# Attention scores from two float32r parts, two heads side by side in the row halves, and a regrouped first stage

## The reference

```
x = layernorm(x + attn(x));  x = layernorm(x + xattn(x, ctx));  x = layernorm(x + ffn(x))
attn:  q, k, v = x W^T + b per head; rotary turn of q and k; softmax(q k^T / 4) v, causal; output projection + bias
xattn: qp = x Wq^T; for each token the context row (of 1601) with the largest qp . ctx is chosen,
       mk, mv = split(ctx[chosen] Wkv^T): one key and one value shared by all heads, 16 wide
       softmax over the chosen rows (one per token, so a row counts as often as it is chosen); projection
ffn:   8 experts (4 x 256 and 4 x 512 wide), top 2 by sigmoid, relu squared, weighted sum
```

## Time and profile before

| engine | busy us | share |
|---|---|---|
| TensorE matmul | 1165.2 | 87% |
| VectorE | 976.3 | 73% |
| ScalarE | 624.5 | 47% |
| GpSimd | 183.0 | 14% |

### The profile page before, as it was taken

One profiled execution on the slowest core, in us unless ns is written; L12 is line 12 of the kernel. 1 busy time (PEld: TensorE's weight loads), 2 busy tenths in 40 slices (PEclk: granted clock), 3 DMA queues, 4 the chain that ended last, 5 costly groups with the idle time before them and its releaser, 6 DMA issues. The chain is left out here.

```text
span 1332.9 us, 18064 instructions
## 1 busy us (share of the span) xinstructions
PE 1165.2 (87%) x6681; PEld 626.0 (47%) x6681; DVE 976.3 (73%) x2195; ACT 624.5 (47%) x838; POOL 183.0 (14%) x165
## 2 busy tenths in 40 slices
PE   6854999999999999964999389999986799999997
PEld 3521233333333333243788112333335489898997
DVE  4474999898899988145799489999918466767675
ACT  1320245756756666841443015666653334444442
POOL 2223111021021100153000430500004000000000
PEclk9785799999999999986999559999987899999999
DMA  6215066920000000030110583200011000000000
GB/s 241 83 60 101 24 69 78 111 30 1 2 2 1 1 1 1 1 132 28 48 48 1 61 98 44 84 1 2 1 50 56 1 1 1 16 1 17 1 16 17
DMA packets 43928, 51.19 MB, mean 38 GB/s; under 512 B 7002, under 2 KB 39258, under 8 KB 43834
## 3 DMA queue, kind: packets, MB, share of 16 engines
q1 hardware_dynamic: 43834, 49.97, 19.2%
HBM read 37.83 MB, written 11.53 MB: 37 GB/s over the span
## 5 line engine op out<-in xcount | busy, mean ns | idle before, releaser
L583 ACT ACTIVATE self_probs<-self_scores 128x1024 f32<-128x1024 f32 (+3 forms) x320 | 273.3, 894 | 199.7 <-PE self_scores L537 198.3
L611 DVE TENSOR_REDUCE self_piece_max<-self_max 128x1 f32<-128x512 f32 x384 | 249.9, 685 | 24.2 <-PE self_max L522 22.8
L522 PE MATMUL self_max<-stack_k,stack_q 96*128 96x512 bf16 (+3 forms) x640 | 209.7, 368 | 21.2 <-DVE self_piece_max L611 8.7
L611 DVE TENSOR_REDUCE cross_piece_max<-cross_max 128x1 f32<-128x512 f32 x256 | 160.6, 683 | 25.2 <-PE cross_max L522 24.5
L583 ACT ACTIVATE cross_probs<-cross_scores 128x1024 f32<-128x1024 f32 x128 | 124.6, 1021 | 108.9 <-PE cross_scores L537 108.8
L537 PE MATMUL self_scores<-stack_q,stack_k 98*128 98x512 bf16 (+3 forms) x640 | 170.7, 351 | 4.3 <-DMA stack_q<-self_shift 3.0
L522 PEld LDWEIGHTS self_max<-stack_k,stack_q 96*128 96x128 bf16 x640 | 61.9, 98 | 202.8 <-DVE self_piece_max L611 104.3
L548 PE MATMUL self_out<-self_probs,V 128*17 128x512 f32 (+3 forms) x1280 | 149.7, 540 | 2.4 <-ACT self_probs L583 2.1
L607 DVE CUSTOM_DVE_ANT_0 self_junk<-self_max,causal_sb 128x128 bf16<-128x128 f32 (+3 forms) x256 | 120.8, 484 | 21.3 <-PE self_max L522 19.8
L1270 ACT ACTIVATE o_tok<-ph 128x512 f32<-128x512 f32 x96 | 57.5, 599 | 143.7 <-PE ph L92 137.5
L92 PE MATMUL py<-w_first,hid_first 128*128 128x256 f32 x384 | 108.7, 283 | 5.7 <-DVE x_sb L1332 5.7
(11 more groups left out here) (209 smaller groups left out, 1772.1 us busy)
## 6 DMA issues: line engine op xcount, KB each, us to landing
stack_q<-qparts SPq DMA_DIRECT2D x96, 64.0 KB, 8.6
stackx<-xparts SPq DMA_DIRECT2D x24, 256.0 KB, 10.9
stack_k<-kparts SPq DMA_DIRECT2D x18, 256.0 KB, 14.3
qparts<-parts SPq DMA_DIRECT2D x8, 384.0 KB, 2.5
kparts<-parts SPq DMA_DIRECT2D x8, 384.0 KB, 2.5
xparts<-xparts_sb SPq DMA_DIRECT2D x8, 384.0 KB, 2.7
cross_raw<-in_w SPq DMA_DIRECT2D x4, 768.0 KB, 4.9
n_raw<-in_w SPq DMA_DIRECT2D x6, 512.0 KB, 4.4
```

Of the source, the lines that this page charges most:

```text
L522: mm = nc.tensor.matmul(slot[:, 0:pc["w"]], pc["lhsT"], pc["rhs"], start=True, stop=True)
L583: nc.scalar.activation(probs[:, i % 3, 2 * pair:2 * pair + 2, st["off"]:C], ps[:, 2 * pair:2 * pair + 2, st["off"]:C], ACT.Exp, scale=SCAL ...
L611: ins = nc.vector.tensor_reduce(to, slot[:, 0:pc["w"]], AX.X, ALU.max)
```

## The change

Parts are float32r (4 bytes) instead of bf16, and two of them do instead of three; `PAIRS` has three products, so a head fills 48 rows. Heads 0 and 2 of a group stand in rows 0 to 47, heads 1 and 3 in rows 64 to 111, and pieces and scores alternate between the halves. The rows of ones are loaded by DMA, not set by GpSimd; a turn needs four DMAs; `po` is cleared by VectorE. In the projections the work goes by pairs, TensorE is one pair ahead with q and k, `parts` and `whole` have four slots, ScalarE rounds once, GpSimd subtracts once, VectorE's `rest` is gone, and the context's keys and values come from one product turned by 13 transposes. The choice stage stores the float32r parts that it has (`qp`), loads `kx` from DRAM in both halves, and packs rows as float32r.

In the head of the file and the projections (GpSimd, TensorE, VectorE):

```diff
-PAIRS = [(0, 0), (0, 1), (1, 0), (0, 2), (2, 0), (1, 1)]
+PAIRS = [(0, 0), (0, 1), (1, 0)]
+HALF = P // 2
...
-        qparts = nc.dram_tensor("qparts", [3, D, T], BF16).ap()
...
+        qparts = nc.dram_tensor("qparts", [2, D, T], F32).ap()
...
-                            pool.wait_ge(p2_ready, n + 1)
-                            if n:
-                                pool.wait_ge(p3_ready, n)
-                            nc.gpsimd.tensor_tensor(parts[:, n % 2, 2], rest[:, n % 2], parts[:, n % 2, 1], ALU.subtract).then_inc(p3_ready, 1)
+                            pool.wait_ge(first_ready, n + 1)
+                            nc.gpsimd.tensor_tensor(parts[:, n % 4, 1], whole[:, n % 4], parts[:, n % 4, 0].bitcast(F32),
+                                                    ALU.subtract).then_inc(parts_ready, 1)
+                        pool.wait_ge(mk_first, 1)
+                        nc.gpsimd.tensor_tensor(mk_parts[:, 1], mkv[0:DK], mk_parts[:, 0].bitcast(F32), ALU.subtract).then_inc(mk_rest, 1)
...
+                        def memory(i):
...
+                            if i < len(mkv_cols):
+                                a, b = mkv_cols[i]
                                 for k in range(KD):
-                                    last = nc.tensor.matmul(pk[0:DK, i % 2, 0:b - a], wkv_sb[:, k, 0:DK], ctx_sb[:, k, a:b],
+                                    last = nc.tensor.matmul(pk[0:2 * DK, i % 2, 0:b - a], wkv_sb[:, k], ctx_sb[:, k, a:b],
                                                             start=(k == 0), stop=(k == KD - 1))
...
                                 for r in range(MT):
+                                    last = nc.tensor.transpose(pk[:, 0, r * 2 * DK:(r + 1) * 2 * DK], mkv[:, r * P:(r + 1) * P],
+                                                               ident[0:2 * DK, 0:2 * DK])
...
+                        products(0)
+                        for p in range(len(turns)):
+                            if p + 1 < len(turns):
+                                products(p + 1)
+                            for n in (2 * p, 2 * p + 1):
+                                values(n)
+                            if 0 <= p - MKV_AT <= len(mkv_cols):
+                                memory(p - MKV_AT)
...
+                            for n in (2 * p, 2 * p + 1):
+                                dve.wait_ge(v_ready, n + 1)
+                                nc.vector.tensor_tensor(V[:, n, :, 0:DK], pv[:, n % 2, 0:D].rearrange("p (h d) -> p h d", h=H),
+                                                        bv_all[:].rearrange("p (h d) -> p h d", h=H), ALU.add).then_inc(v_read, 1)
+                            dve.wait_ge(qk_read, p + 1)
+                            for m in range(KD):
+                                n = KD * p + m
+                                if n >= 4:
+                                    dve.wait_ge(parts_ready, n - 3)
+                                half = (turned, crossed)[m]
+                                nc.vector.tensor_tensor(whole[:, n % 4], half[:, p % 2, 0], half[:, p % 2, 1],
```

In `attention` (SyncE, TensorE) and self attention:

```diff
-                                for b, dst in enumerate(work["shift_to"]):
-                                    sp.dma_start(dst, shift[:, u % 2, b]).then_inc(shift_in[u % 2], 16)
+                                for b, half, dst in work["shift_to"]:
+                                    sp.dma_start(dst.bitcast(F32), shift[half * UR // 2:(half + 1) * UR // 2, u % 2, b].bitcast(F32)).then_inc(shift_in[u % 2], 16)
...
-                            nc.tensor.matmul(po[:], zeros[:, 0:P], zeros[:], start=True, stop=True)
...
-                stack_q = [sb(stage, f"stack_q{g}", [P, NC, GH, C], BF16) for g in range(NG)]
-                stack_k = [sb(stage, f"stack_k{g}", [P, GH, T], BF16) for g in range(NG)]
+                stack_q = [sb(stage, f"stack_q{g}", [P, NC, GH // 2, C], F32R) for g in range(NG)]
+                stack_k = [sb(stage, f"stack_k{g}", [P, GH // 2, T], F32R) for g in range(NG)]
...
+                        for half in range(2):
+                            rows = slice(half * HALF + n * DK, half * HALF + (n + 1) * DK)
+                            mine = slice(g * GH // 2, (g + 1) * GH // 2)
+                            heads = [parts[r].rearrange("(j f i) t -> f i j t", f=2, i=DK)[half][:, mine] for parts, r in ((qparts, a), (kparts, b))]
+                            for c in range(c0, c1):
+                                pairs.append((stack_q[g][rows, c], heads[0][:, :, c * C:(c + 1) * C]))
+                            pairs.append((stack_k[g][rows, :, cols], heads[1][:, :, cols]))
...
+                    if c0 == 0:
+                        for half in range(2):
+                            for j in range(GH // 2):
+                                pairs.append((stack_k[g][half * HALF + KS:half * HALF + KS + 2, j].rearrange("p (n t) -> p n t", t=D),
+                                              ones[0:2].rearrange("p (n t) -> p n t", n=1).to_broadcast([2, T // D, D])))
...
-                        for j in range(GH):
...
+                                for half in range(2):
+                                    rows = slice(half * HALF, half * HALF + KS)
+                                    pieces.append(dict(w=b - a, lhsT=stack_q[g][rows, c, j, q * P:(q + 1) * P],
+                                                       rhs=stack_k[g][rows, j, a:b], row=half * UR // 2 + j * TC + q, at=n,
+                                                       diag=b == end, load=c + 1 if g == 0 else NC + g))
...
-                            keys=lambda j, g=g, kt=kt: stack_k[g][0:KS + 2, j, kt * P:(kt + 1) * P],
-                            queries=lambda j, g=g, c=c, off=off: stack_q[g][0:KS + 2, c, j, off:C],
+                            keys=lambda j, g=g, kt=kt: stack_k[g][j % 2 * HALF:j % 2 * HALF + KS + 2, j // 2, kt * P:(kt + 1) * P],
+                            queries=lambda j, g=g, c=c, off=off: stack_q[g][j % 2 * HALF:j % 2 * HALF + KS + 2, c, j // 2, off:C],
```

In the choice stage and cross attention:

```diff
-                    sel = sb(inner, "sel", [P, 4, FEW], BF16)
-                    row_parts = sb(inner, "row_parts", [P, MT, RW], BF16)
-                    row_rest = sb(inner, "row_rest", [P, MT, 2 * DK])
-                    few_rows = sb(inner, "few_rows", [P, FT, KS + 3])
+                    sel = sb(inner, "sel", [P, 4, FEW], F32R)
...
-                                nc.scalar.copy(parts[:, n % 2, 0], pq[:, n % 2]).then_inc(xp1, 1)
-
-                            def split_rest(n):
-                                act.wait_ge(xrest, n + 1)
-                                nc.scalar.copy(parts[:, n % 2, 1], rest[:, n % 2]).then_inc(xp2, 1)
...
-                                nc.vector.tensor_tensor(rest[:, n % 2], pq[:, n % 2], parts[:, n % 2, 0], ALU.subtract).then_inc(xrest, 1)
-
-                            def split_rest(n):
-                                dve.wait_ge(xp2, n + 1)
-                                nc.vector.tensor_tensor(parts[:, n % 2, 2], rest[:, n % 2], parts[:, n % 2, 1], ALU.subtract).then_inc(xp3, 1)
...
+                stackx = sb(stage, "stackx", [P, NC, H // 2, C], F32R)
+                loads = []
+                for c in range(NC):
+                    pairs = []
+                    for half in range(2):
+                        for n, (a, _) in enumerate(PAIRS):
+                            heads = xparts[a].rearrange("(j f i) t -> f i j t", f=2, i=DK)[half]
+                            pairs.append((stackx[half * HALF + n * DK:half * HALF + (n + 1) * DK, c], heads[:, :, c * C:(c + 1) * C]))
+                        pairs.append((stackx[half * HALF + KS:half * HALF + KS + 1, c].rearrange("p j (n t) -> p (j n) t", t=D),
+                                      ones[0:1].rearrange("p (n t) -> p n t", n=1).to_broadcast([1, H // 2 * C // D, D])))
```

More of the change, by code:

```diff
@@ L234, in _, with products @@
-                        for n, (t, m, c) in enumerate(units):
-                            if c and (t, m) == (0, 0):
+                        def products(p):
+                            t, c = turns[p]
+                            if c and t == 0:
                                 pe.wait_ge(s_x[c], 16 * 3)
-                            pair = n // KD
-                            if pair >= 2 and m == 0:
-                                pe.wait_ge(qk_read, pair - 1)
-                            for k in range(KD):
-                                last = nc.tensor.matmul(pq[:, pair % 2, m], w_sb[:, t, k, m * P:(m + 1) * P],
-                                                        xT_sb[:, k, c * C:(c + 1) * C], start=(k == 0), stop=(k == KD - 1))
+                            if p >= 2:
+                                pe.wait_ge(qk_read, p - 1)
+                            for m in range(KD):
+                                for k in range(KD):
+                                    last = nc.tensor.matmul(pq[:, p % 2, m], w_sb[:, t, k, m * P:(m + 1) * P],
```

(32 more changed lines are left out.)

315 lines of the change are left out of this document (121 added, 194 removed).

## The result

The changed kernel took 1351.05 us (median of four runs, 1346.67 to 1361.31), the kernel before beside it 1331.34. The ratio is 1.0153, 95% interval [1.0083, 1.0222]: slower by 1.5%. The forecast was 1270: it had the wrong sign, and the time lies outside its range of 1248 to 1325. Rival B, the clock, had given 1345. The profiled execution took 1346.86, its span 1345.1, mean granted clock 0.87 (before 0.917). Medians take in all runs, while ratios can leave out some (those over 1.5% above the fastest of their kernel among them), so a ratio is not always the quotient of two medians.

What follows compares the result with a forecast made beforehand. A round trip paced projections; TensorE and VectorE were near their limits in attention. Stage terms -34 + 3 - 22 - 2 - 0.5 + 1.5 - 6 = -60 took 1334.6 to 1274.6, median 1270 us, range 1248 to 1325.

Steps and rivals of the forecast that it cites:

- Rival B: Attention: full steps behind a diagonal or turn run at half speed, 1.2 us each; at 36% slow, 1345 us; chance 0.10.
- Projections, -34: First stage: TensorE becomes the bound and the stage ends at 71 to 72 us instead of 105.3; ends -37 and -22.
- Starts, +3 and +1.5: Starts of self and cross attention: more DMA issues, four DMAs in the first turn and loads of ones lengthen them.
- Self attention's steps: Main part: side-by-side heads cut TensorE's full step from 2.82 to 1.9 us, VectorE is next; -22, ends -37 and +15.
- rival C: Attention: matmuls of the two halves do not overlap; +15 and +7 replace -22 and -6, 1322 or so; chance 0.15.
- a sign of being wrong: Attention steps: prediction wrong if scores matmuls of two halves start 0.2 apart or VectorE still waits for TensorE.
- rival A: Attention: the clock falls part of the time; with 15% of steps at half speed it gains nothing, 1300 us; chance 0.14.
- float32r, priced at nothing: Attention matmuls: float32r costs 0.229 us for 512 columns against 0.23 for bf16; weight loads bring no loss at full widths.
- Cross attention, -6: Cross attention: a unit falls from 12.85 us toward VectorE's 12.2; -6 in all, ends -15 and +7.
- Choice, -0.5: Choice stage: TensorE's shorter first wait gives -2, writing `sel` 4 bytes wide costs +1.5.

Runs made afterwards that it cites:

- The kernel of 32 rows: Kernel before the change with two pairs of parts instead of six, so scores and maxima fill 32 to 35 rows: 1663.53 us, ratio 1.248.
- the zero rows: Changed kernel with each half filled to 62 and 64 rows by zeros that GpSimd and VectorE write, in both attentions: 1337.41 us, ratio 1.002.
- the one with loaded zeros: Changed kernel with zeros loaded by DMA to fill each half to 62 and 64 rows, self attention alone: 1360.76 us, ratio 1.018.

## Why the prediction was wrong

- *Projections, -34.* Measured -32.0. A pair every 5.16 us as forecast, transposes 0.96 us where I took 2. GpSimd's last subtraction took 3.68, the store until the barrier 3.9 instead of 2.3.
- *Starts, +3 and +1.5.* Measured +3.9 and +2.4; self attention's first piece came 11.2 us behind the barrier (11 forecast).
- *Self attention's steps, "if heads run side by side, a pair costs what one does".* They do overlap (884.62, 884.63), so rival C is out. But a pair takes 0.34 (884.62 to 884.97) or 0.23, not always 0.23. Full steps with four pieces take 2.57 in the mean at full speed, close to the 2.55 forecast, but before the change they took 2.68 in self attention; the 2.82 of the prediction is a step of cross attention. In the 103 steps of the main part at full speed in both kernels the gain was 4 us where 22 were forecast for all, and VectorE still waited for TensorE in them, which the prediction had named as a sign of being wrong.
- *The step that failed* is in rival A and B: "Against it: a TensorE at half speed is full again, and full it got its clock back." At half speed TensorE was full, 10.00 of 10 us, and didn't get it back for 100 us; 35 of the 138 steps were slow and took 40 us more. I had read that rule off rows whose matmuls fill 96 rows or more, and carried it to matmuls that fill 48. The kernel of 32 rows (clock 0.56 at 99.8% busy) and the zero rows (165 to 93 us) show what it lacked. The Trainium skill (TensorE: Matmul & The Clock Gate, Why this matters for your kernels) says to keep TensorE busy to have the full clock; the kernel of 32 rows shows that being busy was not enough here.
- *The second step that failed: float32r, priced at nothing* by the earlier trace rows, where TensorE runs at full speed on 128 rows, a load beside each 256 columns. In the row halves it costs some 30 us, half to two thirds of it at full speed (15.5 of 31.0 us in the 138 steps, and 18.3 of 28.1 with filled rows). With bf16 parts in the halves the gain that the prediction counts on is there: 108 steps at full speed in both went from 286.6 before the change to 267.0. How the price splits between longer loads and lost overlap wasn't tried.
- *Rival B came near by luck, in part.* Its mechanism was right, and so were the price of a slow step (1.2; measured 37.9 / 32 = 1.2) and the place: the clock fell at about 222, 273, 382 and 532 us, each time in a narrow step on the diagonal. Its chance of 0.10 was not. But its 1345 (profiled 1346.9) adds 85 us for slow steps (36% of 196, at 1.2) and takes off 39 for faster ones (196 at 0.2); measured were about 41 (35 of the 138 steps and one of cross attention's 62) and 6. The two errors cancel for the most part.
- *Cross attention, -6.* From the first scores to the last product with V it took 204.2 before and 202.3 after. TensorE seemed 97% busy before, yet at full speed a unit took 12.01 us before and 11.79 after (copies of the accumulator on VectorE, mean of seven). In the seven units before the change VectorE was busy 79.80 of 84.10 us (columns as in the earlier trace rows), so little more than 4 us in seven units could come back at all, and 1.5 did:

```profile
860.70:944.80 84.10, 82.90 (x477) 26.44 (x476) 79.80 (x155) 54.27 (x56) 0.00 (x0) 1.00 0.01 2
```

- *Choice, -0.5.* +1.8.

## What to carry to other kernels

A rule about the clock holds for the shape of matmuls it was read from: before you make matmuls fill fewer rows, ask whether stretches at half speed, which here came with the starts and with waits for VectorE, will still end. If a stage doesn't need TensorE's time back, filling many rows cost nothing here and filling fewer cost the clock; where rows are empty, zeros in them can pay (14 us here). Price a new number type in the place where it will stand: at full speed its cost is small per step and runs through all of them. And change one thing at a time: the gain of the first stage was there from the start, under the loss of the second.

## What the hardware showed that was not expected

- TensorE busy 99.8% of 694 us, with scores and pieces of 32 to 35 rows, and at 1.2 GHz for 612 of them.
- Zero rows raise the granted clock (half-speed time 165 to 93 us, and 129 to 63).
- Going between matmuls of 64 rows and of 66 costs about 0.1 us each time, between 65 and 67 nothing (0.31 against 0.23 from start to start).
- A float32r matmul in the row halves costs more than a bf16 one at full speed too: 247.9 against 232.4 us in the same 96 steps.
- The changed kernel's runs spread by 14.6 us (1346.67 to 1361.31), those of the 96-row kernel with the new first stage by 1.2. In cross attention, whose code is the same, half-speed time was 18 us in the changed kernel, 79 in the one with loaded zeros and 45 in the one with bf16 self attention. Which run gets its clock back when is open.
